# Splitting a small softmax chain among the maxima tiles of a two-layer attention kernel, a shorter third Gram tile, and image scores copied by ScalarE

## The chip, the cores and the metric

The kernel runs on one core of one Trainium2 chip. The metric is device time in microseconds of that core. A core has five queues that matter here: TensorE (PE, matrix products; PEld is its weight loads), VectorE (DVE), ScalarE (ACT), GpSimd (POOL) and SyncE (SP, which issues the DMAs). Each works off its own instruction list in order and waits on semaphores that the others raise.

## The reference, cut to what matters

32 batches; per batch 112 queries of 320 features (20 heads of 16) attend to a context of 375 rows of 512 features. There are two layers. Layer 0 attends to 77 text rows and, in a second softmax, to the other 298 rows. Layer 1 takes the last 4 rows as image tokens, the 371 others as text:

```python
probs_t = softmax(q @ k_t * scale);  text_out = probs_t @ v_t
attn_scores = q @ k_ip * scale                      # 112 x 20 x 4 per batch
qsem = l2norm(probs_t @ text_ehs)                   # 512 features per query and head
sem  = qsem @ l2norm(ip_ehs).T
probs_ip = softmax(attn_scores + 0.5 * sem) * side
out = (text_out + probs_ip @ v_ip) @ W_out + b_out + x
```

The kernel never forms `qsem`. With the Gram matrix G = ctx ctxᵀ its norm is a quadratic form in the probabilities, and its products with the image rows come from the last four columns of G. Products need more than one pass of fp32r, so each operand is split in a high part `ch` and a low part `cl`, and a product is hi·hi + hi·lo + lo·hi.

## The kernel before, in words

A planner, `stage_order`, writes one list of stages; every engine's program walks that one list and emits its own part of each stage. So a stage's place in the list fixes its place in five queues at once.

For batch b the list has a stretch here called the maxima window. It has 16 score tiles (`s_max`), eight for layer 0 of batch b+1 and eight for layer 1 of batch b: by turns a wide one of three heads (three matmuls of 375 columns into the PSUM tensor `ST`) and a narrow one of two heads (into `PN`). VectorE takes each tile's row maxima (L1067 and L1068 in layer 0, L1072 in layer 1); the next wide tile may be written only when the last wide one was read, and the same for narrow ones (`free`). After each tile the planner's `between` inserts other work by the tile's number 1 to 16:

- `pieces`: value products `v_mm` (12 matmuls of 320 columns), and the three tiles of G (`g`, 12 matmuls each). ScalarE copies each result out of a bank `R` (three banks, taken in turn). For G it writes the high part `Gh` and the four image columns `g4`; VectorE then writes the low part `Gl` (`g_lo`).
- `last`, which is `finish1` of the batch before: the norm's transposition `ns_T`, `fuse`, `ip_softmax`, the transposition `ip_T` of the image probabilities, their product with the image values `ip_mm`, then `o_T`, `o_mm` and the output. `fuse` is five VectorE operations in a row, each waiting for the one before it, `ip_softmax` three more; an exponential on ScalarE lies between them.
- `rows0`: at tile 10 the 40 row maxima of layer 0 are transposed (`m_T`), copied by ScalarE and split by GpSimd.

Before the change `last` gives a stage after tiles 1, 2, 3, 5, 7, 9 and 10 (`ns_T`, `fuse`, `ip_softmax`, `ip_T`, `ip_mm`, `o_T`, `o_mm`), and `pieces` one after tiles 2, 4, 6, 8, 11, 12, 14 and 16 (value, Gram 0, value, Gram 1, value, Gram 2, value, value). In layer 1 VectorE also copies each tile's image scores into `sip` (L1073). After Gram 2 ScalarE writes the context's high part (`split`), GpSimd its low part, and then GpSimd scales `g4` and ScalarE spreads it over `V1` (`w4`), before it copies the next value product. The window ends with the first scores of batch b+1's layer 0 (L820), `m_T` of layer 1 and the first key product (L707). There are 30 such windows with both layers (b = 1 to 30); the first and the last batch have shorter ones.

Of the kernel before, what the change touches and what calls it, by code (L numbers as in the profile page):

```python
# [60 lines left out]
def stage_order():  # L61
# [190 lines left out]
    def finish1(b):  # L252
        o.add("v_ip", b)
        o.add("ns_copy", b)
        yield
        o.add("ns_T", b)
        in_bank(("ns_T", b), "d_bound", b + 1)
        yield
        o.add("fuse", b)
        yield  # L260
        o.add("ip_softmax", b)
        yield
        o.add("ip_T", b)
        in_bank(("ip_T", b), "ip_T_copied", o.at("ip_T", b))
        yield
        o.add("ip_mm", b)
        in_bank(("ip_mm", b), "ip_added", o.at("ip_mm", b))
        yield
        o.add("o_T", b, 1)
        in_bank(("o_T", b, 1), "o_T_copied", o.at("o_T", b, 1))  # L270
        yield
        o.add("o_mm", b, 1)
        in_bank(("o_mm", b, 1), "x_added", o.at("o_mm", b, 1))
        o.add("out", b)
# [68 lines left out]
    for b in range(B + 1):  # L343
# [68 lines left out]
        def between():  # L412
            count[0] += 1
            if count[0] > 9:
                take(rows0, 1)
            if count[0] in (1, 2, 3, 5, 7, 9, 10):
                take(last, 1)
            if count[0] in (2, 4, 6, 8, 11, 12, 14, 16):
                take(pieces, 1)
            if not b and count[0] > 9:  # L420
                warm("R", (4, 0, 2, 3, 2, 3, 3)[count[0] - 10])
            if b + 1 == B:
                warm("R", 2)
# [8 lines left out]
        if b + 1 == B:  # L432
            take(rows1, 9)
        take(rows0, 9)
        for n in (17, 0, 0, 2, 5, 3, 0):
            take(last, 1)
            if n and b == B:
                warm("R", n)
# [27 lines left out]
def xattn_two_layers(nc, a, out):  # L466
# [3 lines left out]
    with ctx:  # L470
# [6 lines left out]
        def sem(name):  # L477
            return ctx.enter_context(nc.semaphore(name))
# [3 lines left out]
        vipd = nc.dram_tensor("v_ip", [B * NIP, C], fp32, kind="Internal").ap()  # L482

        tx = sb("tx", [128, 4, NT])
        ch = [sb(f"ch{i}", [128, 4, T + 1], f32r) for i in range(2)]
        cl = [sb(f"cl{i}", [128, 4, T + 1], f32r) for i in range(2)]
        wkt = sb("wkt", [128, 4, 384])
        wkh = [sb(f"wkh{i}", [128, 4, n], f32r) for i, n in enumerate((384, 256))]
# [24 lines left out]
                for x in (w2both[:, 1536:1998], w2both[:, 1998:2460], pvt_all[:, 1130:1592])]  # L513
# [50 lines left out]
            sem(n) for n in ("k_mm", "k_hi", "k_rem", "k_mid", "k_mid_act", "k_low", "k_ready"))  # L564
        q_mm, q_hi, q_rem, q_mid, q_low = (sem(n) for n in ("q_mm", "q_hi", "q_rem", "q_mid", "q_low"))
        v_mm, v_copied = (sem(n) for n in ("v_mm", "v_copied"))
        c_hi, c_low, wk_hi, wk_low, c_pads = (sem(n) for n in ("c_hi", "c_low", "wk_hi", "wk_low", "c_pads"))
        g_mm, g_hi, g_lo, g4_scaled, w4_copied = (sem(n) for n in ("g_mm", "g_hi", "g_lo", "g4_scaled", "w4_copied"))
        s_max_mm, s_max_read, m_T, m_hi, m_low = (
            sem(n) for n in ("s_max_mm", "s_max_read", "m_T", "m_hi", "m_low"))  # L570
        s_mm, p_whole, p_round, w_made = (sem(n) for n in ("s_mm", "p_whole", "p_round", "w_made"))
        pv_mm, pv_read, pvT, pvT_read, o_added = (sem(n) for n in ("pv_mm", "pv_read", "pvT", "pvT_read", "o_added"))
        y_mm, w_times_y, ns_added, ns_mm, ns_read, ns_T = (
# [1 line left out]
        d_bound, d_root, fused, fus_less, ip_exp, ip_weights, ip_T, ip_T_copied, ip_mm, ip_added, num_read = (  # L575
            sem(n) for n in ("d_bound", "d_root", "fused", "fus_less", "ip_exp", "ip_weights", "ip_T", "ip_T_copied",
                             "ip_mm", "ip_added", "num_read"))
        o_T, o_T_copied, o_mm, x_added, x1_T, x1_T_copied = (
            sem(n) for n in ("o_T", "o_T_copied", "o_mm", "x_added", "x1_T", "x1_T_copied"))
        kip_mm, kip_hi, kip_rem, kip_mid, kip_low = (sem(n) for n in ("kip_mm", "kip_hi", "kip_rem", "kip_mid", "kip_low"))  # L580
# [53 lines left out]
        kst_before, last_in = {}, {}  # L634
        for j in range(len(nk)):
            kst_before[j], last_in[staged(j)] = last_in.get(staged(j)), j
        def free(w, buffer, what):

            if o.freed[buffer, what]:
                signal, value = o.freed[buffer, what]  # L640
                w.wait_ge(freed_by[signal], value)

        def context(b):

# [24 lines left out]
        def tensor(e):  # L669
            w = Waiter(e)  # L670
            for kind, key in o.stages:
# [108 lines left out]
                elif kind == "g":  # L780
                    b, t = key
                    h, lo, n, first = ch[b % 2], cl[b % 2], ROWS[t], 128 * t
                    r = R[slot["R", ("g", b, t)]]
                    free(w, "R", ("g", b, t))
                    for k in range(4):
                        hk, lk = h[:, k, 128 * t:128 * t + n], lo[:, k, 128 * t:128 * t + n]
                        e.matmul(r[0:n, first:T + 1], hk, h[:, k, first:T + 1], start=k == 0, stop=False)
                        e.matmul(r[0:n, first:T + 1], hk, lo[:, k, first:T + 1], start=False, stop=False)
                        mm = e.matmul(r[0:n, first:T + 1], lk, h[:, k, first:T + 1], start=False, stop=k == 3)
# [183 lines left out]
        def vector(e):  # L973
# [8 lines left out]
            for kind, key in o.stages:  # L982
# [58 lines left out]
                elif kind == "g":  # L1041
# [2 lines left out]
                    ps = R[slot["R", ("g", b, t)]][0:n, 128 * t:T]  # L1044
                    w.wait_ge(g_hi, at("g", b, t))
                    lo = stt(Gl[0:n, q:q + n], ps[:, 0:n], 0.5, Gh[0:n, q:q + n].bitcast(fp32), ALU.mult, ALU.subtract)
                    if gw > n:
                        lo = tt(Gl[0:n, q + n:q + gw], ps[:, n:gw], Gh[0:n, q + n:q + gw].bitcast(fp32), ALU.subtract)
                    lo.then_inc(g_lo, 1)
# [10 lines left out]
                elif kind == "s_max":  # L1060
# [5 lines left out]
                    if l == 0:  # L1066
                        e.reduce_max(m0[:, h0:h0 + n], to[0:S, 0:n, 0:TEXT0], X)  # L1067
                        e.reduce_max(m0[:, H + h0:H + h0 + n], to[0:S, 0:n, TEXT0:T], X).then_inc(s_max_read, 1)  # L1068
                    else:
                        if b >= 2:  # L1070
                            w.wait_ge(fused, b - 1)
                        e.reduce_max(m1[:, h0:h0 + n], to[0:S, 0:n, 0:TEXT1], X)  # L1072
                        e.tensor_copy(sip[b % 2][:, h0:h0 + n, :], to[0:S, 0:n, TEXT1:T]).then_inc(s_max_read, 1)  # L1073
                elif kind == "p_round":
                    n, = key
                    k = at("p_round", n)
# [64 lines left out]
                elif kind == "ns_T":  # L1141
                    b, = key
                    w.wait_ge(pvT_read, at("pvT", b, 1, 1))
                    tt(zq[:], zs[:], zs[:], ALU.mult).then_inc(dve_step, own.one())
                    w.wait_ge(ns_T, b + 1)
                    w.wait_ge(dve_step, own.n)
                    stt(d2[:].rearrange("p (g h) -> p g h", h=GH), zq[:].rearrange("p (g h) -> p g h", h=GH), EPS2 / 2,
                        R[slot["R", ("ns_T", b)]][0:S, 0:128].rearrange("p (h g) -> p g h", g=32)[:, 0:NG], ALU.mult,
                        ALU.max).then_inc(d_bound, 1)
                elif kind == "fuse":  # L1150
                    b, = key
                    f0, f1 = fus
                    w.wait_ge(d_root, b + 1)
                    e.reciprocal(sm[0][:], d2[:]).then_inc(dve_step, own.one())
                    w.wait_ge(dve_step, own.n)
                    tt(f1[:], num[:], sm[0][:].unsqueeze(2).to_broadcast([S, H, NIP]), ALU.mult).then_inc(num_read, 1)
                    w.wait_ge(num_read, b + 1)
                    tt(f0[:], f1[:], sip[b % 2][:], ALU.add).then_inc(fused, 1)
                    w.wait_ge(fused, b + 1)
                    e.reduce_max(sm[1][:], f0[:], X).then_inc(dve_step, own.one())  # L1160
                    w.wait_ge(dve_step, own.n)
                    tt(f1[:], f0[:], sm[1][:].unsqueeze(2).to_broadcast([S, H, NIP]), ALU.subtract).then_inc(fus_less, 1)
                elif kind == "ip_softmax":
                    b, = key
                    f0, f1 = fus
                    w.wait_ge(ip_exp, b + 1)
                    e.reduce_sum(sm[1][:], f0[:], X).then_inc(dve_step, own.one())
                    w.wait_ge(dve_step, own.n)
                    e.reciprocal(sm[2][:], sm[1][:]).then_inc(dve_step, own.one())
                    w.wait_ge(dve_step, own.n)  # L1170
                    if b:
                        w.wait_ge(ip_T, b)
                    w.wait_ge(d_load["small"], 48)
                    stt(f1[:], f0[:], side[:, 0:1], sm[2][:].unsqueeze(2).to_broadcast([S, H, NIP]), ALU.mult,
                        ALU.mult).then_inc(ip_weights, 1)
                elif kind == "ip_mm":
                    b, = key
                    w.wait_ge(ip_mm, b + 1)
                    tt(o_sum[:], R[slot["R", ("ip_mm", b)]][0:S, 0:C], o_sum[:], ALU.add).then_inc(ip_added, 1)

        def scalar(e):
# [5 lines left out]
            for kind, key in o.stages:  # L1187
# [170 lines left out]
                elif kind == "ns_T":  # L1358
# [1 line left out]
                    w.wait_ge(d_bound, b + 1)  # L1360
                    e.activation(d2[:], d2[:], ACT.Sqrt, scale=2.0).then_inc(d_root, 1)
                    e.preload_act_table(ACT.Exp)
                elif kind == "fuse":
                    b, = key
                    w.wait_ge(fus_less, b + 1)
                    e.activation(fus[0][:], fus[1][:], ACT.Exp).then_inc(ip_exp, 1)
# [7 lines left out]
        def gpsimd(e):  # L1374
# [5 lines left out]
            for kind, key in o.stages:  # L1380
                if kind == "w4":
                    b, = key
                    w.wait_ge(g_hi, at("g", b, 2))
                    w.wait_ge(v_mask, 1)
                    e.tensor_tensor(g4[:], g4[:], ninv[:, b, :].unsqueeze(1).to_broadcast([128, 3, NIP]),
                                    ALU.mult).then_inc(g4_scaled, 1)
# [31 lines left out]
                elif kind == "split":  # L1418
                    b, = key
                    for k in range(4):  # L1420
                        w.wait_ge(c_hi, 4 * b + k + 1)
                        less(cl[b % 2][:, k, 0:T], context(b)[:, k, :], ch[b % 2][:, k, 0:T].bitcast(fp32)).then_inc(c_low, 1)
                elif kind == "q":
                    i = at("q", *key)
                    w.wait_ge(q_mid, i)
# [257 lines left out]
```

## Time and profile before

| what | value |
|---|---|
| median of 3 runs | 2545.01 us (2544.8 to 2546.96) |
| the profiled execution | 2546.61 us, its span 2544.8 us |
| granted TensorE clock, mean | 0.995 |
| TensorE busy | 2462.8 us, 97% of the span |
| weight loads (beside the matmuls) | 2130.8 us, 84% |
| VectorE busy | 1636.7 us, 64% |
| ScalarE busy | 1226.3 us, 48% |
| GpSimd busy | 766.4 us, 30% |

The span runs from the first to the last instruction of the program. Matmuls overlap in the records: the start of one lies before the end of the one before it, so what a stage of TensorE takes is read from start to start. A row of a timeline gives start, duration, engine, line, operation, tiles, count and in brackets the idle time before it with its releaser.

### The profile page before, as it was taken

What the parts mean: (1) busy time and instruction counts of PE and PEld (TensorE: products, weight loads), DVE (VectorE), ACT (ScalarE), POOL (GpSimd) and SP (SyncE); (2) the same over time, 40 slices, a digit from 0 to 9 for tenths busy, and PEclk for the clock granted to TensorE, in tenths of its full rate; (3) what the DMA queues carried; (4) which work ended last, traced back from release to release, by engine and by line L of the source; (5) the groups of instructions that cost most, each with busy time, mean ns of one, the idle gap of its engine ahead of it and who ended that gap; (6) DMA issues with size and microseconds to landing.
All of it is one profiled execution on the core that took longest, in us unless ns stands there. A gap on an engine that the chain in (4) does not pass through costs nothing.

```text
span 2544.8 us, 64183 instructions
## 1 busy us (share of the span) xinstructions
PE 2462.8 (97%) x26500; PEld 2130.8 (84%) x26500; DVE 1636.7 (64%) x3217; ACT 1226.3 (48%) x2251; POOL 766.4 (30%) x998
## 2 busy tenths in 40 slices
PE   7899999999999999999999999999999999999998
PEld 7788888888888888888888888888888888888877
DVE  4465667766667666667656677666677556676665
ACT  3355444455444455444554444554444554444543
POOL 3133233233233232233332323332332332332322
PEclk9999999999999999999999999999999999999999
DMA  9775446674456754456655466745566645566611
GB/s 215 138 107 86 88 84 99 107 117 74 86 86 96 117 89 86 89 90 112 103 87 89 85 101 103 107 75 89 97 95 108 91 81 88 90 95 105 94 26 21
DMA packets 371689, 241.45 MB, mean 95 GB/s; under 512 B 131947, under 2 KB 365243, under 8 KB 371388
## 3 DMA queue, kind: packets, MB, share of 16 engines
q1 hardware_dynamic: 371398, 237.35, 57.1%
q8 instruction: 210, 3.44, 0.7%
q14 instruction: 81, 0.66, 0.1%
HBM read 171.35 MB, written 64.59 MB: 93 GB/s over the span
## 4 chain that ended last, share of the span: by engine, by line
PE 77%; DVE 13%; POOL 4%; DMA 2%; issue 2%; ACT 1%; SPq 1%; DVEq 0%; POOLq 0%; ACTq 0%
PE ST L820 7%; PE R L886 6%; PE R L762 5%; PE PN L859 5%; PE R L775 4%; PE R L776 4%; PE R L707 4%; DVE m L1068 4%; PE R L708 4%; POOL w L1444 3%; PE R L944 3%; PE R L778 3%; PE PN L904 3%; PE R L710 3%; PE R L889 3%; PE R L891 3%
## 5 line engine op out<-in xcount | busy, mean ns | idle before, releaser
L1444 POOL TENSOR_TENSOR w<-w 128x448 f32<-128x448 f32 (+1 forms) x256 | 328.8, 1284 | 378.8 <-DVE w L977 360.6
L980 DVE SCALAR_TENSOR_TENSOR w<-p,pr 128x1344 f32<-128x1344 f32 x160 | 296.0, 1850 | 166.7 <-ACT pr L1330 151.0
L1302 ACT ACTIVATE p<-ST 128x1344 f32<-128x1344 f32 x260 | 335.4, 1290 | 101.8 <-PE ST L823 97.4
L886 PE MATMUL R<-pr,Gh 128*128 128x448 f32 (+1 forms) x960 | 366.2, 381 | 0.8 <-issue 0.8
L977 DVE TENSOR_TENSOR rem<-R,kst 128x298 f32<-128x298 f32 (+2 forms) x180 | 89.4, 497 | 428.3 <-ACT kst L1185 428.3
L977 DVE TENSOR_TENSOR w<-R,w 128x448 f32<-128x448 f32 (+1 forms) x480 | 281.5, 619 | 68.8 <-PE R L891 57.8
L1378 POOL TENSOR_TENSOR kst<-rem,kst 128x298 bf16<-128x298 f32 (+2 forms) x180 | 147.9, 822 | 534.5 <-ACT kst L1185 293.2
L775 PE MATMUL R<-wvh,ch 128*128 128x320 f32 (+3 forms) x896 | 303.4, 339 | 1.1 <-DVE rem L977 1.1
L776 PE MATMUL R<-wvh,cl 128*128 128x320 f32 (+3 forms) x896 | 277.9, 310 | 0.0
L820 PE MATMUL ST<-Qs,Ks 100*128 100x112 bf16 (+1 forms) x3520 | 229.3, 214 | 10.3 <-ACT p L1302 3.5
L820 PEld LDWEIGHTS ST<-Qs,Ks 100*128 100x128 bf16 (+1 forms) x3520 | 188.1, 98 | 48.6 <-issue 13.9
L707 PE MATMUL R<-ch,wkh 128*128 128x298 f32 (+1 forms) x636 | 215.3, 338 | 2.8 <-POOL cl L1378 2.8
L778 PE MATMUL R<-wvl,ch 128*128 128x320 f32 (+3 forms) x672 | 208.5, 310 | 0.0
L1330 ACT ACTIVATE pr<-ST 128x1344 fp32r<-128x1344 f32 x160 | 205.1, 1282 | 0.0
L708 PE MATMUL R<-cl,wkh 128*128 128x298 f32 (+1 forms) x636 | 199.7, 314 | 0.0
L886 PEld LDWEIGHTS R<-pr,Gh 128*128 128x128 f32 (+1 forms) x960 | 175.8, 183 | 23.8 <-issue 7.4
L1185 ACT ACTIVATE pvt<-PN 128x112 f32<-128x112 f32 (+2 forms) x260 | 88.7, 341 | 215.0 <-PE PN L908 161.2
L889 PE MATMUL R<-pr,Gl 128*115 128x448 f32 (+1 forms) x480 | 176.2, 367 | 0.0
L891 PE MATMUL R<-pr,Gl 128*128 128x448 f32 (+1 forms) x480 | 175.7, 366 | 0.0
L1072 DVE TENSOR_REDUCE m<-ST 112x3 f32<-112x1113 f32 x128 | 167.9, 1312 | 8.0 <-PE ST L804 8.0
L1185 ACT ACTIVATE V<-R 128x320 f32<-128x320 f32 (+3 forms) x161 | 68.0, 436 | 213.2 <-PE R L779 213.2
L775 PEld LDWEIGHTS R<-wvh,ch 128*128 128x128 f32 (+3 forms) x896 | 161.7, 180 | 9.3 <-DVE rem L977 1.3
(221 smaller groups left out, 5930.9 us busy)
## 6 DMA issues: line engine op xcount, KB each, us to landing
Ks<-k_split SPq DMA_DIRECT2D x384, 140.6 KB, 5.7
Ks<-k_split SPq DMA_DIRECT2D x384, 93.8 KB, 8.0
w<-in_ctxT SPq DMA_DIRECT2D x31, 750.0 KB, 9.5
k_split<-kst SPq DMA_DIRECT2D x64, 281.2 KB
k_split<-kst SPq DMA_DIRECT2D x64, 223.5 KB, 2.9
Qs<-q_split SPq DMA_DIRECT2D x64, 210.0 KB, 8.6
q_split<-qst SPq DMA_DIRECT2D x128, 84.0 KB, 2.4
Qs<-q_split SPq DMA_DIRECT2D x64, 140.0 KB, 8.7
```

What stands on the lines that cost most here:

```text
L707: e.matmul(r[:, 0:t1 - t0], wh[:, k, c0:c0 + 128], h[:, k, t0:t1], start=k == 0, stop=False)
L708: e.matmul(r[:, 0:t1 - t0], wh[:, k, c0:c0 + 128], lo[:, k, t0:t1], start=False, stop=False)
L775: e.matmul(r[0:n, 0:C], h[:, k, :], wh[:, k, :], start=k == 0, stop=False)
L776: e.matmul(r[0:n, 0:C], lo[:, k, :], wh[:, k, :], start=False, stop=False)
L778: e.matmul(r[0:n, 0:C], h[:, k, :], wl[:, k, :], start=False, stop=False)
L820: e.matmul(ST[:, u, S * h:S * h + S], Ks[l][0:m, GH * g + h, 128 * u:128 * u + 128], Qs[l][0:m, GH * g + h, :], start=True, stop=True)
L886: e.matmul(r[0:nj, 0:QW], Gh[0:ROWS[u], q:q + nj], x[0:ROWS[u], QW * u:QW * u + QW], start=u == 0, stop=False)
L889: e.matmul(r[0:nj, 0:QW], Gl[0:ROWS[u], q:q + nj], x[0:ROWS[u], QW * u:QW * u + QW], start=False, stop=False)
L977: return e.tensor_tensor(to, x, y, op)
L980: return e.scalar_tensor_tensor(out=to, in0=x, scalar=s, in1=y, op0=op0, op1=op1)
L1302: e.activation(to.rearrange("p (u q) -> p u q", u=3), st, ACT.Exp).then_inc(p_whole, 1)
L1444: e.tensor_tensor(first, first, w2[n % 2][0:ROWS[j], QW * j:QW * j + QW], ALU.add).then_inc(ns_added, 1)
```

## The change

Steps of `finish1` that were two stages become eight, and `between` hands out one after every tile but the 13th, so that the image attention's eight VectorE operations stand at tiles 2 to 9, `ip_T` at 10, `ip_mm` at 11, `o_T` at 12 and `o_mm` at 14. The pieces stand after tiles 2, 3, 5, 6, 8, 11, 13 and 15. The third Gram tile is made by 8 matmuls: four hi·hi ones of 124 columns (four more hold the low parts of the image rows, which GpSimd copies behind `ch`), and four lo·hi ones into the same bank; VectorE adds the missing terms. Layer 1's image scores are copied out of PSUM by ScalarE, and a maxima tile's bank is free only when both have read it.

```diff
@@ finish1
-        o.add("fuse", b)
-        yield
-        o.add("ip_softmax", b)
-        yield
+        for step in ("root_inverse", "sem", "fuse", "fuse_max", "fuse_less", "ip_sum", "ip_inverse", "ip_softmax"):
+            o.add(step, b)
+            yield
@@ between
-            if count[0] in (1, 2, 3, 5, 7, 9, 10):
+            if b + 1 == B:
+                take(last, (0, 1, 5, 3, 0, 1, 0, 1, 0, 1, 1)[count[0]])
+            elif count[0] != 13:
                 take(last, 1)
-            if count[0] in (2, 4, 6, 8, 11, 12, 14, 16):
+            if count[0] in ((2, 3, 5, 6, 8, 11, 13, 15) if 0 < b < B - 1 else (2, 4, 6, 8, 11, 12, 14, 16)):
                 take(pieces, 1)
@@ free
                 w.wait_ge(freed_by[signal], value)
+                if signal == "s_max_read" and image_reads[value]:
+                    w.wait_ge(sip_read, image_reads[value])
@@ tensor, g
+                    if t == 2:
+                        w.wait_ge(c_image, b + 1)
+                        for k in range(4):
+                            e.matmul(r[0:n, first:T + 1 + NIP], h[:, k, first:first + n], h[:, k, first:T + 1 + NIP],
+                                     start=k == 0, stop=k == 3)
+                        for k in range(3):
+                            e.matmul(r[0:n, 0:T + 1 - first], lo[:, k, first:first + n], h[:, k, first:T + 1], start=k == 0,
+                                     stop=False)
+                        e.matmul(r[0:n, 0:T + 1 - first], lo[:, 3, first:first + n], h[:, 3, first:T + 1], start=False,
+                                 stop=True).then_inc(g_mm, 1)
+                        continue
@@ vector, g
+                    if t == 2:
+                        lo.then_inc(dve_step, own.one())
+                        r, made = R[slot["R", ("g", b, t)]], own.n
+                        tt(g4[0:n, 2, :], r[0:n, T + 1:T + 1 + NIP], g4[0:n, 2, :], ALU.add).then_inc(dve_step, own.one())
+                        w.wait_ge(dve_step, made)
+                        lo_ = Gl[0:n, q:q + n]
+                        tt(lo_, r[0:n, 0:n], lo_.bitcast(fp32), ALU.add)
+                        w.wait_ge(dve_step, own.n)
+                        tt(g4[0:n, 2, :], r[0:n, n:n + NIP], g4[0:n, 2, :], ALU.add).then_inc(g_lo, 1)
+                        continue
@@ vector, s_max of layer 1
-                        if b >= 2:
-                            w.wait_ge(fused, b - 1)
-                        e.reduce_max(m1[:, h0:h0 + n], to[0:S, 0:n, 0:TEXT1], X)
-                        e.tensor_copy(sip[b % 2][:, h0:h0 + n, :], to[0:S, 0:n, TEXT1:T]).then_inc(s_max_read, 1)
+                        e.reduce_max(m1[:, h0:h0 + n], to[0:S, 0:n, 0:TEXT1], X).then_inc(s_max_read, 1)
@@ scalar
+                elif kind == "s_max" and key[1] == 1:
+                    b, l, h0, wide = key
+                    n, to = (3, ST) if wide else (2, PN)
+                    w.wait_ge(s_max_read, at("s_max", *key))
+                    if b >= 2:
+                        w.wait_ge(fused, b - 1)
+                    copy(sip[b % 2][:, h0:h0 + n, :], to[0:S, 0:n, TEXT1:T]).then_inc(sip_read, 1)
@@ gpsimd
-                    w.wait_ge(g_hi, at("g", b, 2))
+                    w.wait_ge(g_lo, at("g", b, 2))
...
+                    w.wait_ge(c_low, 4 * (b + 1))
+                    e.tensor_copy(ch[b % 2][:, :, T + 1:T + 1 + NIP], cl[b % 2][:, :, T - NIP:T]).then_inc(c_image, 1)
```

## Rows read from the trace of the kernel before

**Rows 1.** The page, busy time by engine over the whole span
```profile
PE 2462.8 (97%) x26500; PEld 2130.8 (84%) x26500; DVE 1636.7 (64%) x3217; ACT 1226.3 (48%) x2251; POOL 766.4 (30%) x998
```
**Rows 2.** TensorE's timeline, one quiet maxima window: start us, duration us, line, operation
```profile
1411.75 0.53 PE L802 MATMUL ST<-Ks,Qs 96*112 96x375 bf16 x2
...
1415.20 0.37 PE L802 MATMUL PN<-Ks,Qs 96*112 96x375 bf16 x1
...
1419.49 0.37 PE L802 MATMUL PN<-Ks,Qs 96*112 96x375 bf16 x1 [0.56 <-DVE m L1068]
...
1422.09 0.70 PE L971 MATMUL R<-vbd,prT 80*112 80x320 f32 x2
1422.63 0.32 PE L802 MATMUL PN<-Ks,Qs 96*112 96x375 bf16 x1
...
1424.33 0.48 PE L802 MATMUL ST<-Ks,Qs 96*112 96x375 bf16 x2
...
1425.10 0.33 PE L802 MATMUL PN<-Ks,Qs 96*112 96x375 bf16 x1
...
1425.42 0.26 PE L811 MATMUL R<-ident_sb,m 112*40 112x112 f32 x1
1425.94 1.30 PE L944 MATMUL R<-wo,x1T 128*112 128x320 f32 x4 [0.26 <-ACT x1T L1185]
...
1427.62 0.48 PE L802 MATMUL ST<-Ks,Qs 96*112 96x375 bf16 x2
...
1429.87 0.32 PE L802 MATMUL PN<-Ks,Qs 96*112 96x375 bf16 x1
...
1431.35 0.48 PE L802 MATMUL ST<-Ks,Qs 96*112 96x375 bf16 x2
...
1437.22 0.38 PE L707 MATMUL R<-ch,wkh 128*128 128x298 f32 x1
```
**Rows 3.** TensorE's timeline, begin and end of another, disturbed window
```profile
874.54 0.53 PE L802 MATMUL ST<-Ks,Qs 96*112 96x375 bf16 x2
...
900.48 0.38 PE L707 MATMUL R<-ch,wkh 128*128 128x298 f32 x1
```
**Rows 4.** VectorE's timeline in the quiet window
```profile
1412.47 0.40 DVE L1067 TENSOR_REDUCE m<-ST 112x3 f32<-112x231 f32 x1
...
1415.06 0.27 DVE L1154 RECIPROCAL sm<-d 112x20 f32<-112x20 f32 x1
...
1416.35 0.39 DVE L1067 TENSOR_REDUCE m<-ST 112x3 f32<-112x231 f32 x1
...
1417.65 0.23 DVE L1167 TENSOR_REDUCE sm<-fus 112x20 f32<-112x80 f32 x1
...
1418.44 0.31 DVE L1067 TENSOR_REDUCE m<-PN 112x2 f32<-112x154 f32 x1
...
1419.36 0.28 DVE L980 SCALAR_TENSOR_TENSOR Gl<-R,Gh 128x128 fp32r<-128x128 f32 x1
...
1425.46 1.30 DVE L1072 TENSOR_REDUCE m<-ST 112x3 f32<-112x1113 f32 x1
1426.68 0.16 DVE L1073 COPY sip<-ST 112x12 f32<-112x12 f32 x1
1426.76 0.92 DVE L1072 TENSOR_REDUCE m<-PN 112x2 f32<-112x742 f32 x1
```
**Rows 5.** ScalarE's timeline in the quiet window
```profile
1417.83 0.54 ACT L1185 ACTIVATE Gh<-R 128x128 fp32r<-128x128 f32 x2 [0.76 <-PE R L789]
...
1418.97 0.26 ACT L1185 ACTIVATE prT<-R 80x112 f32<-80x112 f32 x1 [0.54 <-PE R L964]
...
1425.72 0.26 ACT L1185 ACTIVATE mrem<-R 40x112 f32<-40x112 f32 x1
...
1436.11 0.44 ACT L1185 ACTIVATE V<-g 128x240 f32<-128x240 f32 x1 [2.61 <-POOL g L1385]
```
**Rows 6.** Waits of the weight loads over the span: us in total, times, longest us
```profile
PEld PN L802 <- DVE m L1068: 38.9, 65, 1.0
```

More of the change, by code:

```diff
@@ L434, in stage_order @@
         take(rows0, 9)
-        for n in (17, 0, 0, 2, 5, 3, 0):
+        for n in (17, 0, 0, 0, 0, 0, 0, 0, 0, 2, 5, 3, 0):
             take(last, 1)
@@ L484, in xattn_two_layers @@
         tx = sb("tx", [128, 4, NT])
-        ch = [sb(f"ch{i}", [128, 4, T + 1], f32r) for i in range(2)]
+        ch = [sb(f"ch{i}", [128, 4, T + 1 + NIP], f32r) for i in range(2)]
         cl = [sb(f"cl{i}", [128, 4, T + 1], f32r) for i in range(2)]
@@ L566, in xattn_two_layers @@
         v_mm, v_copied = (sem(n) for n in ("v_mm", "v_copied"))
-        c_hi, c_low, wk_hi, wk_low, c_pads = (sem(n) for n in ("c_hi", "c_low", "wk_hi", "wk_low", "c_pads"))
+        c_hi, c_low, c_image, wk_hi, wk_low, c_pads = (
+            sem(n) for n in ("c_hi", "c_low", "c_image", "wk_hi", "wk_low", "c_pads"))
         g_mm, g_hi, g_lo, g4_scaled, w4_copied = (sem(n) for n in ("g_mm", "g_hi", "g_lo", "g4_scaled", "w4_copied"))
-        s_max_mm, s_max_read, m_T, m_hi, m_low = (
-            sem(n) for n in ("s_max_mm", "s_max_read", "m_T", "m_hi", "m_low"))
+        s_max_mm, s_max_read, sip_read, m_T, m_hi, m_low = (
+            sem(n) for n in ("s_max_mm", "s_max_read", "sip_read", "m_T", "m_hi", "m_low"))
         s_mm, p_whole, p_round, w_made = (sem(n) for n in ("s_mm", "p_whole", "p_round", "w_made"))
@@ L577, in xattn_two_layers @@
                              "ip_mm", "ip_added", "num_read"))
+        root_inverted, ip_max, ip_summed, ip_inverted = (
+            sem(n) for n in ("root_inverted", "ip_max", "ip_summed", "ip_inverted"))
         o_T, o_T_copied, o_mm, x_added, x1_T, x1_T_copied = (
@@ L636, in xattn_two_layers @@
             kst_before[j], last_in[staged(j)] = last_in.get(staged(j)), j
+        image_reads = [0]
+        for kind, key in o.stages:
+            if kind == "s_max":
+                image_reads.append(image_reads[-1] + key[1])
         def free(w, buffer, what):
@@ L1149, in vector @@
                         ALU.max).then_inc(d_bound, 1)
+                elif kind == "root_inverse":
+                    b, = key
+                    w.wait_ge(d_root, b + 1)
+                    e.reciprocal(sm[0][:], d2[:]).then_inc(root_inverted, 1)
+                elif kind == "sem":
+                    b, = key
+                    f1 = fus[1]
+                    w.wait_ge(root_inverted, b + 1)
+                    tt(f1[:], num[:], sm[0][:].unsqueeze(2).to_broadcast([S, H, NIP]), ALU.mult).then_inc(num_read, 1)
                 elif kind == "fuse":
@@ L1152, in vector @@
                     f0, f1 = fus
[L1153 to L1156, printed above, removed]
                     w.wait_ge(num_read, b + 1)
+                    w.wait_ge(sip_read, 8 * (b + 1))
                     tt(f0[:], f1[:], sip[b % 2][:], ALU.add).then_inc(fused, 1)
+                elif kind == "fuse_max":
+                    b, = key
                     w.wait_ge(fused, b + 1)
-                    e.reduce_max(sm[1][:], f0[:], X).then_inc(dve_step, own.one())
-                    w.wait_ge(dve_step, own.n)
-                    tt(f1[:], f0[:], sm[1][:].unsqueeze(2).to_broadcast([S, H, NIP]), ALU.subtract).then_inc(fus_less, 1)
+                    e.reduce_max(sm[1][:], fus[0][:], X).then_inc(ip_max, 1)
+                elif kind == "fuse_less":
+                    b, = key
+                    f0, f1 = fus
+                    w.wait_ge(ip_max, b + 1)
+                    tt(f1[:], f0[:], sm[1][:].unsqueeze(2).to_broadcast([S, H, NIP]), ALU.subtract).then_inc(fus_less, 1)
+                elif kind == "ip_sum":
+                    b, = key
+                    w.wait_ge(ip_exp, b + 1)
+                    e.reduce_sum(sm[1][:], fus[0][:], X).then_inc(ip_summed, 1)
+                elif kind == "ip_inverse":
+                    b, = key
+                    w.wait_ge(ip_summed, b + 1)
+                    e.reciprocal(sm[2][:], sm[1][:]).then_inc(ip_inverted, 1)
                 elif kind == "ip_softmax":
@@ L1165, in vector @@
                     f0, f1 = fus
[L1166 to L1170, printed above, removed]
+                    w.wait_ge(ip_inverted, b + 1)
                     if b:
@@ L1362, in scalar @@
                     e.preload_act_table(ACT.Exp)
-                elif kind == "fuse":
+                elif kind == "s_max" and key[1] == 1:
[5 more added lines that the diff above has]
+                    copy(sip[b % 2][:, h0:h0 + n, :], to[0:S, 0:n, TEXT1:T]).then_inc(sip_read, 1)
+                elif kind == "fuse_less":
                     b, = key
```

## The prediction

> **What bounds the kernel now.** I read the page first: TensorE is busy for 2462.8 of 2544.8 us [rows 1], so what matters is TensorE's own work and the few places where it stands still. Then the waits of the weight loads: the largest that names another engine is a narrow score tile waiting for VectorE's maxima, 65 times, 38.9 us [rows 6]. That is the maxima window, so I read each queue's timeline there [rows 2, 4, 5]. Time is counted from the window's first matmul (1411.75). It ends with the first key product at 1437.22, after 25.47 us; a disturbed window took 25.94 [rows 3].
>
> In this window two queues are equally full. A score tile is three or two matmuls of 0.16 us, and then VectorE needs 1.30 (wide) or 0.92 (narrow) for its maxima in layer 0 (1416.35 to 1417.65, 1418.44 to 1419.36) and 1.22 or 0.84 in layer 1 (an operation's duration less the 0.08 that the next one overlaps) [rows 4]. TensorE's own work fills the rest. Where VectorE stays with the five operations of `fuse` (1415.06 to 1416.35, 1.29) and the three of `ip_softmax` (1417.65 to 1418.44, 0.79), TensorE later waits: 0.56 before the narrow tile at 1419.49 [rows 2]. All waits of TensorE in the window that go back to this chain I estimate at 1.5 us. So it is a hand-over game: what counts is not the sum of either queue but which stage stands how many tiles behind the one that it needs.
>
> **The change, part by part.**
>
> *The third Gram tile.* From 1429.87 to 1431.35 are 1.48 us; less the narrow tile's 0.32 (1425.10 to 1425.42) that is 1.16 for 12 matmuls, 0.10 each [rows 2]. Four go: 0.40 per batch. Four extra columns in four of them cost between nothing and 0.06 in all; I take nothing. VectorE gets three more operations, between 0.3 and 1.0 us (three small copies of the kind of 0.16, or three like the 0.28 of Gl) [rows 4]; the next reader of that bank is three bank users away and tile 14 comes over 2 us later, so I take 0 on the path. GpSimd's extra copy and its wait for `g_lo` delay `w4`, for which ScalarE already waits 2.61 us [rows 5]; in the new list ScalarE's copy for tile 14 stands behind it and releases tile 16, with about 1 us to spare. Cost 0 to 0.5, taken as 0.
>
> *Image scores to ScalarE.* VectorE loses eight copies that cost it 0.08 each (1426.68 to 1426.76) [rows 4]. ScalarE gains eight of 0.16 to 0.26 (the same copy on VectorE, and ScalarE's small PSUM copy at 1418.97) [rows 4, 5]; I take 0.17. What is queued behind them is what matters: each stands in ScalarE's list at its tile and waits until VectorE has finished that tile, and everything after it on ScalarE waits too.
>
> *Order.* I walk the new list with the durations of the rows; TensorE first. Tiles 1 and 2, `ns_T` and a value product take 0.48 + 0.32 + 0.11 + 1.77 (1427.62 to 1429.87 less 0.48), so tile 3 starts at 2.68 and Gram 0 at 3.16. Its result comes 2.26 after its start (1415.20 to 1417.83 less 0.37), at 5.42, and ScalarE's copies take 0.60 more: 6.02 [rows 2, 5].
>
> VectorE starts at 0.72 (1412.47). Tile 1, the two operations on the norm, tile 2, the reciprocal, tile 3 and `sem` are 1.30 + 0.38 (what 1412.47 to 1415.06 holds besides the two tiles) + 0.92 + 0.19 + 1.30 + 0.16 = 4.25, so 4.97; a split step costs its row's 0.23 to 0.28 less 0.08. The low part of Gram 0 now comes here, and it isn't ready before 6.07: 1.1 us idle. Then Gram 0 (0.51), tile 4, `fuse`, tile 5, `fuse_max`, tile 6, `fuse_less` (0.51 + 0.92 + 0.16 + 1.30 + 0.16 + 0.92 + 0.16 = 4.13) end at 10.20. Gram 1 stood at the same place, and its copies on ScalarE come only after the exponential that needs `fuse_less`: 10.28 + 0.04 + 0.27 + 0.50 = 11.09, VectorE idle for 0.85 again. Gram 1 0.40, tile 7 1.30, `ip_sum` 0.15, tile 8 0.92: 13.86. Tile 10 needs tile 8 read, so TensorE writes it at 13.97, where it was at 13.35 before (1425.10). Without those two pauses TensorE would be there at about 12.6 by its own work.
>
> From there it gets worse. `ip_softmax` is at tile 9, `ip_T` at tile 10. VectorE does `ip_inverse` 0.20, tile 9 1.22, `ip_softmax` 0.30 after 13.86: 15.58, with the signal 15.62. TensorE has written tile 10 and `m_T` by 14.39: **a new gap of 1.23**. Before, a tile and a half lay between them. Next, `ip_mm` at tile 11 needs `prT` from ScalarE, whose list there reads: image scores of tile 10, two copies of `m_T`, `prT`. VectorE ends tile 10 at 16.42; 0.04 + 0.14 + 0.35 + 0.26 + 0.04 give 17.24 (durations 0.26 at 1425.72 and 0.26 at 1418.97, overlaps taken off) [rows 5]. TensorE is ready at 15.62 + 0.10 + 0.48 = 16.20: **a second gap of 1.05**.
>
> Behind it TensorE has only its own work: `ip_mm` 0.54 (1422.09 to 1422.63), Gram 2 0.76, tile 12 0.32, `o_T` 0.29 (1424.33 to 1425.10 less 0.48), tile 13 0.48, value 1.77, tile 14 0.32, `o_mm` 1.68 (1425.94 to 1427.62), tile 15 0.48, value 1.77: tile 16 at 25.66 [rows 2]. No value product follows tile 16 any more, so the `m_T` after the first scores waits for its maxima: 25.66 + 0.48 + 0.04 + 0.92 + 0.04 = 27.14, and the key product starts at 27.24.
>
> ScalarE's strict order decides the second gap. The Trainium skill, "PSUM — Partial Sum Buffer", section "Engine vs sequencer instructions", says the same of all three: "ScalarE/VectorE/GpSimdE queues are strict FIFO." If ScalarE could take `prT` first, that gap would be about 0.3 and the window 26.5 us.
>
> **The sum.** 27.24 against 25.47 is +1.77 for a quiet window. Against the disturbed one (25.94) it is +1.30, since VectorE's late start there falls into the new pause of 1.1. I take 1.65, nearer the quiet kind: 30 windows make +49.5. The two short batches save the Gram's 0.40 each: -0.8. After the window TensorE is full again (97%), so nothing there takes up the delay, and each later transfer starts with it. The profiled execution is 2546.6 (span 2544.8, 1.8 around it), so the sum is 2595.3 for such a run; against the median 2545.0 it is 2593.7, say **2594**.
>
> **The rivals.**
>
> *Milder: slower, but only by the first gap.* If ScalarE reaches `prT` early (its copies hidden by a later tile 11), the second gap of 1.05 goes: 26.19, +0.6 in the mean, about 2562. For it: ScalarE is 48% busy [rows 1]. Against: what precedes `prT` waits for VectorE, not for ScalarE.
>
> *The Gram tile alone counts.* New waits as long as the old ones: 32 times -0.40 is -13, 2532. For it: both kinds of wait are consequences of the two queues being equally full, and the walk could overstate them if VectorE got ahead. *The two cancel*: 2545.
>
> *Faster: the waits go.* Its mechanism is the breaking up of the chain at tiles 2 to 4: VectorE never stays away from the maxima for more than one small operation, saves the pauses between dependent operations (2.08 us for eight of them now, 1.3 split) and eight copies (0.64), and TensorE's 1.5 us go along with the Gram's 0.40: -1.9 each, 2545 - 57 - 1 = 2487. It decides from the point where the new gaps together stay under 1.9 us; my walk has 1.23 + 1.05 + 0.56 at the window's end, besides some 1.4 before tile 10. The Trainium skill, "TensorEngine Tiling (Array Packing)", section "PSUM Bottleneck", speaks for this side: use both ScalarE and VectorE to empty PSUM. By that rule the hand-over gets faster. The rows bear it out for VectorE's 0.08 a copy only; each bank now has two readers in series.
>
> **How the numbers follow.** The forecast (2575 to 2612) 0.58, the milder one 0.17, cancelling 0.05, Gram alone 0.12, waits gone 0.08. This kernel's runs tell 0.2% (5 us) from no change. So slower 0.75, same 0.05, faster 0.20. The upper end, 2612, adds the unknown ends: 0.5 us a window for `w4` and ScalarE's copies. The lower end, 2535, reaches to the Gram case; left out are the fastest case, half of the Gram case, and a tail above, near 0.2.
>
> **What would show it.** In the new trace: maxima windows of about 27.2 us from the first score tile to the first key product; TensorE idle for about 1.2 us before `ip_T`, 1 us before `ip_mm`, 0.5 before the second `m_T`; `prT` directly behind an image-score copy that waited for VectorE; VectorE idle before the low parts of Gram 0 and 1; Gram 2 in 0.76 us. It would be wrong if `ip_T` came with no gap (VectorE ahead of TensorE by a tile), or if windows lasted under 25 us. It would be wrong in size if ScalarE's copies took over 0.3 us, or if the stages after the window shrank.

## The result, and the profile after

The changed kernel takes 2670.99 us (median of 4 runs, 2669.73 to 2671.33) against 2545.86 us for the kernel before (4 runs): 1.0491 times as long, 95% interval 1.0472 to 1.0509. That is 125 us more, where 49 were forecast. The direction was right, the size two and a half times too small, and the time lies outside the range (2535 to 2612).

The page of the changed kernel, with the line that answers to [rows 1]: TensorE is busy 79 us longer, though it has 128 matmuls fewer.

```profile
span 2668.8 us, 64280 instructions
PE 2542.2 (95%) x26372; PEld 2192.7 (82%) x26372; DVE 1614.8 (61%) x3057; ACT 1261.6 (47%) x2507; POOL 777.4 (29%) x1030
```

The view of the cores gives the reason for that: the mean granted TensorE clock was 0.995 in the kernel before. (The page's row of the clock doesn't show it. In tenths per slice it reads 9 in all 40 slices, before and after.)

```profile
core 0: 2668.8 us, clock 0.958
```

TensorE's timeline of one of the 30 windows answers to [rows 2] (start, duration, line):

```profile
1480.79 0.53 PE L824 MATMUL ST<-Ks,Qs 96*112 96x375 bf16 x2
...
1494.65 0.37 PE L824 MATMUL PN<-Ks,Qs 96*112 96x375 bf16 x1 [0.31 <-DVE m L1100]
...
1495.02 0.26 PE L833 MATMUL R<-ident_sb,m 112*40 112x112 f32 x1
1496.30 0.26 PE L986 MATMUL R<-ident_sb,fus 112*80 112x112 f32 x1 [1.02 <-DVE fus L1002]
...
1497.85 1.38 PE L993 MATMUL R<-vbd,prT 80*112 80x320 f32 x2 [0.77 <-issue]
1498.56 1.35 PE L799 MATMUL R<-ch 128*115 128x124 f32 x4
1499.71 0.78 PE L802 MATMUL R<-ch,cl 128*115 128x120 f32 x3
...
1510.79 0.26 PE L833 MATMUL R<-ident_sb,m 112*20 112x112 f32 x1 [0.52 <-DVE m L1102]
1510.91 0.37 PE L718 MATMUL R<-ch,wkh 128*128 128x298 f32 x1
```

Up to `ip_T` this is the forecast window: tile 10 at 13.86 us (forecast 13.97), `ip_T` at 15.51 (15.62) after a wait of 1.02 (1.23), `ip_mm` at 17.06 (17.24) after one of 0.77 (1.05), each counted from 1480.79. From there the forecast is off: the key product comes at 30.12 instead of 27.24. `ip_mm` takes 0.71 from start to start instead of 0.54, and the third Gram tile 1.9 instead of 0.76. The view by stretches shows why (columns: busy time and count of TensorE, its weight loads, VectorE, ScalarE, GpSimd, then the granted clock, DMA share and GB/s):

```profile
1480.80:1494.00 13.20, 12.74 (x87) 11.58 (x84) 11.03 (x33) 5.66 (x14) 0.79 (x1) 1.00 0.75 146
1494.00:1498.00 4.00, 1.90 (x11) 0.88 (x9) 3.88 (x6) 0.90 (x5) 0.39 (x1) 0.90 0.01 2
1498.00:1500.00 2.00, 2.00 (x8) 1.56 (x9) 0.93 (x2) 0.18 (x1) 0.66 (x2) 0.50 0.02 4
1500.00:1504.00 4.00, 4.00 (x18) 3.62 (x18) 2.65 (x6) 2.46 (x9) 2.47 (x3) 0.50 0.03 7
1504.00:1511.00 7.00, 6.48 (x47) 5.48 (x47) 3.82 (x5) 2.03 (x8) 1.43 (x4) 1.00 0.19 50
```

Between 1494 and 1498 TensorE is busy for 1.90 of 4 us. Near the end of that stretch, at 1497.2, the granted clock falls to 0.5 (1.2 GHz in place of 2.4) and stays there until 1504.0, in the very stretch where TensorE has nothing to wait for and every matmul counts. In 29 of the 30 windows the clock falls like this; the mean of a window is then 0.84 to 0.94, and the window lasts 28.7 to 31.2 us. It stays at 1.00 only in the first.

The kernel before had such falls already, though rarely: in two of its 30 windows, behind waits of 0.67 and 0.56 us. They lasted 27.64 us, against 25.5 for the others. This is one of the two:

```profile
255.90:283.50 27.60, 25.88 (x168) 22.22 (x164) 23.46 (x54) 9.77 (x28) 5.58 (x9) 0.94 0.44 91
```

ScalarE's timeline shows the second wait as it was forecast. `prT` stands behind the image scores of tile 10 and the two copies of `m_T`:

```profile
1497.03 0.18 ACT L1229 ACTIVATE sip<-PN 112x8 f32<-112x8 f32 x1 [0.86 <-DVE m L1102]
1497.10 0.25 ACT L1229 ACTIVATE mrem<-R 40x112 f32<-40x112 f32 x1
1497.26 0.24 ACT L1229 ACTIVATE ms<-R 40x112 bf16<-40x112 f32 x1
1497.49 0.26 ACT L1229 ACTIVATE prT<-R 80x112 f32<-80x112 f32 x1
```

VectorE's shows the two pauses before the low parts of Gram 0 and Gram 1, forecast as 1.1 and 0.85:

```profile
1486.88 0.29 DVE L1002 SCALAR_TENSOR_TENSOR Gl<-R,Gh 128x128 fp32r<-128x128 f32 x1 [1.12 <-ACT g L1229]
...
1491.77 0.29 DVE L1002 SCALAR_TENSOR_TENSOR Gl<-R,Gh 128x128 fp32r<-128x128 f32 x1 [0.72 <-ACT g L1229]
```

And TensorE's waits over the whole span (us, times, longest): 30 times, 1.0 us each, before `ip_T`.

```profile
PE R L986 <- DVE fus L1002: 30.8, 30, 1.0
PE R L833 <- DVE m L1102: 16.6, 31, 0.9
PE ST L824 <- DVE m L1100: 14.4, 32, 0.7
PE R L993 <- issue: 14.3, 24, 0.8
PE PN L824 <- DVE m L1100: 9.8, 33, 0.3
```

### The profile page after: what moved, and what is told of

It reads as the page before. It is cut to its first block, busy times and chain, and to the rows that moved or that the text cites. A ratio compares the mean times of both kernels' runs of the same rounds, so it can differ in the third digit from the quotient of the medians.

```text
span 2668.8 us, 64280 instructions
## 1 busy us (share of the span) xinstructions
PE 2542.2 (95%) x26372; PEld 2192.7 (82%) x26372; DVE 1614.8 (61%) x3057; ACT 1261.6 (47%) x2507; POOL 777.4 (29%) x1030
## 4 chain that ended last, share of the span: by engine, by line
PE 74%; DVE 14%; POOL 4%; ACT 2%; issue 2%; DMA 2%; SPq 1%; DVEq 0%; POOLq 0%; ACTq 0%
PE ST L842 6%; PE R L908 5%; PE PN L881 5%; PE R L773 5%; DVE m L1100 4%; PE R L718 4%; PE R L786 4%; PE R L787 4%; PE R L719 4%; POOL w L1497 3%; PE R L966 3%; PE PN L926 3%; PE R L789 3%; DVE m L1102 3%; PE R L721 3%; PE R L911 3%
## 5 line engine op out<-in xcount | busy, mean ns | idle before, releaser
L786 PE MATMUL R<-wvh,ch 128*128 128x320 f32 (+3 forms) x896 | 317.1, 354 | 0.0
L787 PE MATMUL R<-wvh,cl 128*128 128x320 f32 (+3 forms) x896 | 287.3, 321 | 0.0
L789 PE MATMUL R<-wvl,ch 128*128 128x320 f32 (+3 forms) x672 | 215.3, 320 | 0.0
L786 PEld LDWEIGHTS R<-wvh,ch 128*128 128x128 f32 (+3 forms) x896 | 172.3, 192 | 10.1 <-issue 0.7
L787 PEld LDWEIGHTS R<-wvh,cl 128*128 128x128 f32 (+3 forms) x896 | 171.4, 191 | 2.3
```

Source lines behind the costliest of these rows:

```text
L786: e.matmul(r[0:n, 0:C], h[:, k, :], wh[:, k, :], start=k == 0, stop=False)
L787: e.matmul(r[0:n, 0:C], lo[:, k, :], wh[:, k, :], start=False, stop=False)
L789: e.matmul(r[0:n, 0:C], h[:, k, :], wl[:, k, :], start=False, stop=False)
```

## The experiments

Theory A: the new waits cost what the walk of the queues gives, some 1.5 us a window, and they let the clock fall, which costs the rest. Each run is compared with the kernel before on the same chip (2540 to 2541 us there), so ratios are what to compare. The edits are shown shortened, with comments that the kernels don't have; where one lists tiles, these are the numbers after which a stage stands, not code.

**Spare work in the two waits.** The changed kernel; the spare matmuls write where nothing is read.

```diff
+        warm("R", 8)
         o.add("ip_T", b)
...
+        warm("R", 8)
         o.add("ip_mm", b)
```

> The changed kernel, with eight spare matmuls of 128 columns on TensorE ahead of ip_T and eight ahead of ip_mm in each of the 30 full windows; they fill waits and compute nothing that is used. Theory A (the two new waits of about 1.0 us leave TensorE idle, its granted clock falls to 0.5 for some us, and the work behind them runs at half speed): the clock stays at 1.0 in the windows, a window lasts 27.2 to 27.5 us as its waits alone make it, and the whole takes about 2600 us (mean clock over 0.985). Rival B (the two further microseconds of a window come from the changed work itself: two readers of a bank in series, the other Gram tile, ScalarE's queue): the spare matmuls change nothing or cost time, 2670 to 2700 us.

2627.49 us, ratio 1.0346 (1.0328 to 1.0363), clock 0.995. So the clock is back, and 1.4% with it, but the median window is 28.56 us, not 27.2 to 27.5, and the time is 27 us above the 2600 expected. The trace has the reason: eight spare matmuls are sixteen of 0.11 us each, more than the wait.

```profile
1468.84 1.96 PE L744 MATMUL R<-wkt 128*128 128x128 f32 x16
1470.63 0.26 PE L999 MATMUL R<-ident_sb,fus 112*80 112x112 f32 x1
```

Five and three of them instead:

> The changed kernel with five spare matmuls ahead of ip_T and three ahead of ip_mm. In the run before each spare matmul came out as two of 0.115 us, so eight of them were longer than the wait (16 in 1.8 us) and added about 1.3 us to a window. Five and three (1.15 and 0.69 us) fit into the waits. Theory A (waits plus clock): clock 1.0 through the windows, windows of 27.2 to 27.4 us, the whole 2588 to 2596. Rival (the spare matmuls didn't cost anything, the windows of 28.6 are what the change's work takes at full clock): 2625.

2582.60 us, ratio 1.0170 (1.0148 to 1.0192), clock 0.996. A window of it, in the same view as above:

```profile
1432.20:1459.40 27.20, 25.75 (x183) 22.57 (x176) 22.28 (x49) 11.01 (x37) 5.73 (x10) 1.00 0.48 88
```

Median window 27.08 us, with the clock at 1.00 in 28 of the 30. That is the changed kernel at full clock, where the walk had said 27.24; the total is 5 us under what was expected. Of the 4.91% the clock makes 3.2 points (some 82 us), and 1.7 points (43 us) are what the change costs at full clock, waits above all. The spare matmuls take away none of the work and write only where nothing is read. They do take a turn of the `R` banks, so this run alone doesn't separate the two; the next run (one turn in place of two, the same time) and the two kinds of window in the run after it do.

At full clock `ip_mm` and the third Gram tile are short again, 0.39 and 1.01 us from start to start, where they were 0.71 and 1.92:

```profile
1449.27 0.79 PE L1006 MATMUL R<-vbd,prT 80*112 80x320 f32 x2 [0.15 <-ACT prT L1249]
1449.66 0.77 PE L812 MATMUL R<-ch 128*115 128x124 f32 x4
...
1450.67 0.33 PE L837 MATMUL PN<-Ks,Qs 96*112 96x375 bf16 x1
```

Five ahead of `ip_T` alone, none ahead of `ip_mm`:

```diff
+        warm("R", 5)
         o.add("ip_T", b)
```

> The changed kernel with five spare matmuls ahead of ip_T alone; the wait ahead of ip_mm stays empty. It asks which of the waits lets the clock fall. If the waits add up: the remaining ones (0.5 and 0.3 at tiles 9 and 10, 0.8 to 1.0 ahead of ip_mm) are too little, the clock stays and the time is that of the run with five and three, 2583. If the one ahead of ip_mm is enough by itself: 2640 to 2670.

2583.59 us, ratio 1.0175 (1.0157 to 1.0193), clock 0.997. One filled wait is enough. The other stays, 30 times, and in 29 of the 30 windows the clock doesn't fall for it (whether filling the second alone would do as well was not run):

```profile
PE R L1004 <- issue: 22.9, 30, 0.9
PE ST L835 <- DVE m L1111: 14.3, 32, 0.7
```

**The parts one by one**, each put alone into the kernel before. First the order of stages (steps, tiles, pieces as in the change):

> The kernel before with the order alone: eight steps at tiles 2 to 9, ip_T at 10, ip_mm at 11, o_T at 12, o_mm at 14, pieces at 2, 3, 5, 6, 8, 11, 13, 15. Image scores stay on VectorE, Gram 2 has its 12 matmuls. Theory A: the wait before ip_T stays (1.3 us), the one before ip_mm nearly goes, since no image-score copy stands ahead of prT on ScalarE; windows +1.5 us at a full clock (2592), and if one long wait and the two before it are enough for the clock to fall, 2620 to 2650. Rival B (ScalarE's copies are the main cause): under 2580.

2637.90 us, ratio 1.0397 (1.0353 to 1.0440), clock 0.971. Its windows come in two kinds, about 26.9 us where the clock stays (11 of them) and most often 30.1 where it falls (19), from the same program with the same waits:

```profile
815.10:842.10 27.00, 24.48 (x168) 21.07 (x164) 22.42 (x54) 10.55 (x29) 5.55 (x9) 1.00 0.44 86
893.70:923.90 30.20, 27.68 (x171) 23.99 (x164) 22.61 (x54) 10.70 (x29) 5.55 (x9) 0.89 0.35 73
```

The order alone is thus already over the edge, though not in every window. The 3.2 us between the two kinds are the price of one fall, with no spare matmul in play. The wait before `ip_T` in the two kinds of window, the one at 1.00 and the one at 0.89, is the same to the hundredth:

```profile
830.77 0.26 PE L999 MATMUL R<-ident_sb,fus 112*80 112x112 f32 x1 [1.15 <-DVE fus L1015]
909.38 0.27 PE L999 MATMUL R<-ident_sb,fus 112*80 112x112 f32 x1 [1.15 <-DVE fus L1015]
```

Then the Gram tile (8 matmuls, three more VectorE operations):

```diff
-                    for k in range(4):      # hi*hi, hi*lo, lo*hi: 12 matmuls of 120 columns
+                    for k in range(4):      # hi*hi with the image rows' low parts: 124 columns
...
+                    for k in range(4):      # lo*hi: 120 columns
```

> The kernel before with the eight-matmul Gram tile alone (old order, image scores on VectorE). Theory A: TensorE is full and four matmuls of 0.10 us go per batch, 32 x 0.40: -13 us, 2532. Rival: the time is handed to a wait for VectorE, 2545; or three more VectorE operations and the later w4 cost more than the matmuls save: 2550 to 2560.

2537.54 us, ratio 0.9987 (0.9977 to 0.9996): about -3 us, not -13. The weight loads' waits show where the rest went. Narrow tiles wait for VectorE's copy of the image scores 61 times, 23.4 us, in place of 31 times, 7.8 us, in the kernel before:

```profile
PEld PN L837 <- DVE m L1113: 40.5, 64, 1.1
PEld PN L837 <- DVE sip L1121: 23.4, 61, 0.6
```

```profile
PEld PN L802 <- DVE sip L1073: 7.8, 31, 0.3
```

The first fence is that run, the second the kernel before. In the old order VectorE sets the pace of the last tiles, and 0.4 us less on TensorE is about 0.4 us more waiting: the median window at full clock went from 25.50 to 25.47 us only, while the tile itself became 0.40 us shorter (1.30 to 0.90).

Then the image scores on ScalarE:

> The kernel before with the image scores copied by ScalarE alone (old order, 12 matmuls). Theory A: ScalarE takes each copy only when VectorE is through with the tile, so the copy of o_T into x1T, which stands behind the copy for tile 9, is late and o_mm at tile 10 waits about 2 us for it instead of 0.3; windows +2.4 us, 2615, and up to 2650 if the clock falls as well. Rival (VectorE gets 0.64 us a window back and ScalarE is idle half the time, so the move is free): 2525 to 2545.

2629.58 us, ratio 1.0345 (1.0320 to 1.0370), clock 0.982. Windows at full clock last 27.5 to 28.0 us (six of them; the walk had 2.4 us more than before, the median is 2.15 more), most of those where it falls 29.1 to 29.7:

```profile
1626.00:1655.30 29.30, 26.37 (x172) 21.85 (x164) 22.43 (x46) 10.80 (x36) 5.57 (x9) 0.94 0.41 79
1706.80:1734.40 27.60, 24.64 (x172) 20.88 (x164) 22.40 (x46) 10.81 (x36) 5.56 (x9) 1.00 0.44 84
```

The wait is the one expected, `o_mm` for `x1T`, which ScalarE copies behind the image scores. The first line is this run, the second the kernel before:

```profile
PE R L979 <- ACT x1T L1249: 53.4, 30, 1.8
```

```profile
PE R L944 <- ACT x1T L1185: 8.2, 30, 0.6
```

So moving eight small copies to an engine that is idle half of the time costs as much as 2 us a window in this order, and the clock on top. The three parts do not add up to the whole: order and copies alone cost 4.0 and 3.5 points, all together 4.9. Each of the two already lets the clock fall by itself, and that price is not paid twice.

**The place of the stages.** The changed kernel with `ip_T` and what follows it later:

```diff
-ip_T 10, ip_mm 11, o_T 12, o_mm 14
+ip_T 11, ip_mm 13, o_T 14, o_mm 16
```

> The changed kernel with ip_T, ip_mm, o_T and o_mm at tiles 11, 13, 14 and 16 in place of 10, 11, 12 and 14: two tiles between ip_softmax and ip_T and between ip_T and ip_mm. Theory A (distance in tiles sets the wait): both waits under 0.5 us, windows of 26.8 us by the same walk where the clock stays, and the clock falls less often: 2575 to 2620. Rival (the waits come from VectorE and ScalarE being full, wherever the stages stand): the waits move along, 2650 or more.

2644.83 us, ratio 1.0414 (1.0384 to 1.0443), clock 0.969: 25 us above what was expected. Undisturbed windows are 26.5 us (0.6 shorter than with the changed order at full clock), but three in four still lose the clock and last 28.6. TensorE's waits over the whole span:

```profile
PE ST L837 <- ACT sip L1249: 38.4, 44, 1.4
PE R L786 <- DMA xT<-in_xT: 27.1, 29, 1.6
```

The two waits of the forecast are gone. Another has come: wide tiles now wait for ScalarE's copy of the image scores, up to 1.4 us at once, because the bank that they want has two readers and the second is late. Both sides get a half: the distance takes away the waits that it was meant to, and in this order one moves to the bank's second reader (1.0 us at tile 11), and the clock still falls at it or within 2.6 us behind it in three windows of four. The second row is a foretaste of the load that two runs below are about.

All of the chain earlier instead, pieces unchanged:

```diff
-sem 3, fuse 4, fuse_max 5, fuse_less 6, ip_sum 7, ip_inverse 8, ip_softmax 9, ip_T 10, ip_mm 11, o_T 12, o_mm 14
+sem 3, fuse 3, fuse_max 3, fuse_less 4, ip_sum 5, ip_inverse 6, ip_softmax 7, ip_T 9, ip_mm 11, o_T 13, o_mm 16
```

> The changed kernel, all its parts, with the chain placed anew: ns_T 1, root_inverse 2, sem, fuse and fuse_max 3, fuse_less 4, ip_sum 5, ip_inverse 6, ip_softmax 7, ip_T 9, ip_mm 11, o_T 13, o_mm 16. Theory A: no long wait ahead of ip_T and ip_mm, the clock stays at 1.0, windows of 25.4 us, 2535 to 2545: the whole loss was the place of two stages. Rival (two readers of a bank and ScalarE's longer queue cost by themselves): 2570 or more.

2557.04 us, ratio 1.0070 (1.0049 to 1.0092), clock 0.995, every window 25.2 us (25.4 expected). With the same parts and only other places, 4.2 of the 4.9 points are gone. The total was missed by 12 to 22 us all the same: the windows are shorter than before the change, and the kernel is slower. The stretches between windows had grown, from 51.3 to 52.1 us in the mean. And waits alone don't decide about the clock: TensorE still waits 43 times for ScalarE's copy of the image scores here (30.7 us, the longest 1.4), and the clock stays at 1.00 in all 30 windows.

The kernel before with the split chain placed like that, and the pieces too:

```diff
+PIECES = 2, 3, 5, 6, 7, 9, 12, 14
```

> The kernel before, chain split in eight steps, placed as in the run with the early chain (1, 2, 3, 3, 3, 4, 5, 6, 7, 9, 11, 13, 16), pieces after tiles 2, 3, 5, 6, 7, 9, 12, 14; image scores on VectorE, 12 matmuls. Theory A, by the same walk of the queues: windows of 23.9 us against 25.2, that is -1.4 x 30 = -42, about 2500. Rival (both queues are full at 25.4 us, no order helps): 2535 to 2545.

2522.89 us, ratio 0.9928 (0.9908 to 0.9948). Windows of 23.86 us, as the walk gave; but of the 42 us expected only 18 arrive. The stretches between the windows have grown here too, to 52.2 us. The waits name it:

```profile
PE R L786 <- DMA xT<-in_xT: 33.2, 29, 2.0
```

The query product waits for its input, 29 times, 1.1 us in the mean. SyncE's timeline shows the load of `xT` directly behind the output, which waits for `o_mm`, now at tile 16:

```profile
1348.06 0.34 SPq L1666 DMA_DIRECT2D out<-x  x1
1348.45 0.42 SPq L1591 DMA_DIRECT2D xT<-in_xT  x1
```

With that load issued before the window, behind the one of `xn`, and taken out of its old place:

```diff
-        if b + 1 < B:
-            o.add("xT", b + 1)
...
+        if b + 2 < B:
+            o.add("xT", b + 2)
```

> The placed version (chain split, placed anew, image scores on VectorE, 12 matmuls), whose windows lasted 23.9 us but whose stretches between windows grew by 0.96 us, because the load of xT stands on SyncE behind the output's DMA and that waits for o_mm at tile 16. Here xT of the next batch is issued before the window. Theory: the 33 us that the query product waited for xT go, about 2490 to 2497. Rival (the stretch grew for another reason, the load only happened to end last): 2515 to 2525.

**2481.44 us, ratio 0.9773 (0.9758 to 0.9787)**, 9 us under the lower end of what was expected. This version beats both kernels: 2.3% under the kernel before. Its window:

```profile
1377.80:1401.70 23.90, 23.77 (x168) 21.02 (x164) 22.06 (x54) 9.76 (x28) 5.56 (x9) 1.00 0.42 87
```

TensorE is busy for 23.77 of 23.90 us. (The eight-matmul Gram tile was not run in this order.) And the same with ScalarE copying the image scores:

> The same with ScalarE copying the image scores, nothing else changed. Theory A (two readers of a bank in series, and what stands on ScalarE behind each copy): windows of 25.2 us in place of 23.9 by the walk of the queues, +1.3 x 30 = 39, about 2530 to 2540, at a full clock. Rival (the copies only hurt where prT stands right behind one): within 5 us of the version with the copies on VectorE.

2516.99 us, ratio 0.9911 (0.9894 to 0.9927), 13 us under the lower end of what was expected; windows of 24.9 us, and, besides the first, three of 26.4 in which the clock fell. The copies on ScalarE cost 1.0 us a window in this order, against the 1.3 of the walk. `ip_mm` does not wait for `prT` here, though `prT` still stands right behind a copy; the score tiles wait, 37 us in all. The longest such wait is for a copy that stands on ScalarE behind the splitting of the context, so it isn't the copy's own 0.15 us that costs:

```profile
1415.93 1.73 ACT L1251 ACTIVATE ch<-w 128x375 fp32r<-128x375 f32 x4
1417.57 0.15 ACT L1251 ACTIVATE sip<-PN 112x8 f32<-112x8 f32 x1
```

Theory A stands, its size too high by a quarter.

## Why the prediction was wrong, point by point

- **That the maxima window is where it is decided**, and that two equally full queues trade waits there: right. The stretches between windows stayed at 51.1 us in the mean (51.3 before).
- **The walk up to tile 10, the wait before `ip_T`, the wait before `ip_mm`**: right to 0.3 us each (1.02 for 1.23, 0.77 for 1.05), as was the small one before the second `m_T` (0.52). That VectorE would stand idle before the low parts of two Gram tiles: right (1.12 and 0.72 us). These steps named the mechanism.
- **"Behind it TensorE has only its own work"** is the step that failed. Its terms (`ip_mm` 0.54, Gram 2 0.76, ten more up to the key product) are durations from rows at full clock, [rows 2], and the sum took for granted that the clock would be the same behind a stretch of two waits. It was 0.5 for 6.8 us (1497.2 to 1504.0 in the window shown), and this part of the window took 13.1 us instead of 10.0. No rival asked what longer waits would do to the clock, though two windows of the kernel before, which none of its rows shows, had lost it for 3.4 us each. That is the term left out: 3.0 us in a typical window (30.08 against 27.08), 82 us in all by the run with the waits filled.
- **The terms that were in the sum**: +49 us, of which the chip has 43 (ratio 1.017). Taken with the quiet window alone, the walk's 27.24 became 27.08. Part of this closeness is luck, since small errors cancel: `ip_mm` came 0.2 us before its time in the walk, and `ip_mm` with Gram 2 took 1.40 us at full clock, not 1.30 (Gram 2 alone 1.01, not 0.76, with the matmuls of 124 columns at 0.15 us each).
- **The Gram tile counted as -0.4 us everywhere.** The saving is real wherever TensorE was traced at full clock (1.30 to 0.90 in the old order, 1.41 to 1.01 in the new), and behind the last wait of the walk it counts. The rival that gave it alone -13 us overlooked that in the old order VectorE has the pace there; it measured -3.
- **The unknown costs** were well bounded: ScalarE's copy of image scores takes 0.18 us (0.17 taken), VectorE's three new operations 0.4 to 0.6 (0.3 to 1.0), and in the window shown none of them sets the end.
- **The faster rival** said that breaking up the chain lets VectorE and TensorE run side by side, 2487 us. The mechanism exists: with the chain split and placed otherwise the windows are 23.86 us (2523 us in all), and with `xT` loaded earlier 2481. That this lies near 2487 is chance, for that run has neither the copies on ScalarE nor the shorter Gram tile, and the load's move was in nobody's sum. Of the change, the splitting was the part for it; the places, and the copies on ScalarE, were against it. Its turning point (new gaps together under 1.9 us) was not tested as such.

## What to carry to other kernels

Splitting a chain into steps paid here only where the stages that read its results stood far enough behind: with one tile between `ip_softmax` and `ip_T` TensorE waited 1.0 us in every window, with two it didn't, and the same held between `ip_T` and `ip_mm`, where ScalarE copies in between. Walk the queues with durations from the timeline; at full clock it came within 0.3 us of a window here. Then ask of each wait that the walk leaves how idle TensorE is around it, and price what follows at half its clock as well. A few spare matmuls in the wait, shorter than the wait, tell on the chip, in one run, which of the two costs you are paying. And look at what else stands behind a stage that you move late, the DMAs of the next batch first of all.

## What the runs showed of the hardware that was not expected

- Near the end of a stretch of 4 us in which TensorE was busy for 1.90 us, the clock fell to 0.5 (1.2 GHz) and stayed there for 6.8 us, though TensorE was full again from 1498 on. One microsecond of idling decided it: with the first of two waits filled, the clock stayed at 1.00 in 29 of 30 windows (0.997 in the mean of the run).
- It is not a fixed consequence of the program: with the order alone, windows with the same waits had the full clock (26.9 us) or lost it (30.1 us) within one execution. What decides between the two is open.
- A mean clock of 0.995 hides falls: the kernel before has two windows with one (27.64 against 25.5 us).
- Spare fp32 matmuls of 128 columns come out as two of 0.11 us each.
